# A Swin block on one core: epsilon moves into the summed squares, and the residual copy moves to another round

## The reference, cut to what matters

```python
def _ln(x, w, b):
    mu = x.mean(-1, keepdims=True)
    var = x.var(-1, keepdims=True)
    return (x - mu) / jnp.sqrt(var + 1e-05) * w + b
...
y = _ln(x, norm1_w, norm1_b)            # then roll and cut into windows
qkv = win @ qkv_w.T
attn = softmax(q @ k.T * scale + bias + mask)
x = shortcut + (attn @ v) @ proj_w.T + proj_b
z = _ln(x, norm2_w, norm2_b)
return x + gelu(z @ fc1_w.T + fc1_b) @ fc2_w.T + fc2_b
```

## Time and profile before

| what | value |
|---|---|
| median of 3 runs | 2193.38 us (2191.87 to 2196.89) |
| the profiled execution: time / span | 2191.34 us / 2189.5 us |
| PE / PEld busy | 2140.3 us (98%) / 1667.7 us (76%) |
| DVE / ACT / POOL busy | 1780.1 (81%) / 1545.3 (71%) / 1772.9 us (81%) |
| transfers | 165.86 MB, 76 GB/s |
| mean granted PE clock | 0.993 |

### The profile page before, as it was taken

How to read it: one execution, slowest core, us unless ns; L and a number is a source line. 1 busy time by engine, 2 the same in 40 slices (tenths; PEclk the granted TensorE clock), 3 DMA queues, 4 the chain that set the end, 5 groups by cost and what they waited for, 6 DMA issues and landing times.

```text
span 2189.5 us, 148006 instructions
## 1 busy us (share of the span) xinstructions
PE 2140.3 (98%) x62790; PEld 1667.7 (76%) x62790; DVE 1780.1 (81%) x3231; ACT 1545.3 (71%) x2435; POOL 1772.9 (81%) x1687
## 2 busy tenths in 40 slices
PE   6999999999999999999999999999999999999997
PEld 3777777777777777777777777777777777777775
DVE  5788888888888888888888888888888888888874
ACT  4577777677677777767777776776777777777774
POOL 5788888888888888888888888888888888888874
PEclk8999999999999999999999999999999999999999
DMA  4232233222323332232323223233223333322321
GB/s 111 65 78 78 75 75 76 77 77 76 79 74 76 76 76 77 75 79 76 77 76 76 77 75 77 78 75 79 75 77 77 76 77 76 77 76 76 77 70 32
DMA packets 178587, 165.86 MB, mean 76 GB/s; under 512 B 21144, under 2 KB 152458, under 8 KB 178074
## 3 DMA queue, kind: packets, MB, share of 16 engines
q1 hardware_dynamic: 178074, 157.60, 28.0%
HBM read 28.99 MB, written 25.77 MB: 25 GB/s over the span
## 4 chain that ended last, share of the span: by engine, by line
PE 88%; DVE 4%; issue 3%; ACT 2%; SPq 2%; DMA 1%; DVEq 0%; POOL 0%; ACTq 0%; POOLq 0%
PE O L758 14%; PE S L722 11%; PE ST L744 10%; PE M L766 9%; PE ST L738 9%; PE M L829 9%; PE M L851 8%; PE M L814 5%; PE M L798 5%; PE M L784 4%; PE M L859 2%; PE S L726 2%; SPq L274 1%; DVE nm L582 1%; ACT gl L445 1%
## 5 line engine op out<-in xcount | busy, mean ns | idle before, releaser
L326 POOL TENSOR_TENSOR nmd<-diag,nm 121x392 f16<-121x392 f16 x1024 | 900.3, 892 | 288.1 <-DVE nm L582 234.1
L582 DVE TENSOR_REDUCE nm<-S 121x8 f16<-121x392 f32 x1024 | 574.3, 561 | 225.7 <-PE S L722 138.3
L426 ACT ACTIVATE pT<-ST 113x392 f32<-113x392 f32 x1024 | 506.9, 496 | 229.7 <-PE ST L744 224.9
L758 PEld LDWEIGHTS O<-vx,pT 113*49 113x49 f32 x16384 | 548.6, 126 | 45.1 <-issue 6.1
L758 PE MATMUL O<-vx,pT 113*49 113x18 f32 x16384 | 522.2, 196 | 3.8 <-issue 1.9
L722 PE MATMUL S<-kp,qp 128*49 128x49 f16 x16384 | 390.7, 186 | 11.0 <-DVE nm L582 7.9
L738 PE MATMUL ST<-qp,kp 128*49 128x49 f16 x16384 | 387.0, 185 | 2.4 <-issue 2.3
L722 PEld LDWEIGHTS S<-kp,qp 128*49 128x49 f16 x16384 | 313.0, 103 | 93.1 <-issue 55.5
L744 PE MATMUL ST<-nmd,shiftw 121*49 121x392 f16 x2048 | 354.4, 342 | 0.2 <-POOL nmd L326 0.2
L738 PEld LDWEIGHTS ST<-qp,kp 128*49 128x49 f16 x16384 | 324.8, 103 | 10.2 <-issue 2.3
L407 ACT ACTIVATE hl<-M 128x784 f16<-128x784 f32 x128 | 105.5, 824 | 309.1 <-PE M L784 229.3
(11 more groups left out here) (90 smaller groups left out, 3369.2 us busy)
## 6 DMA issues: line engine op xcount, KB each, us to landing
qp<-hl SPq DMA_DIRECT2D x1024, 49.0 KB
kp<-hl SPq DMA_DIRECT2D x1024, 49.0 KB
xin<-in_x SPq DMA_DIRECT2D x256, 98.0 KB
out<-res SPq DMA_DIRECT2D x256, 98.0 KB
kp<-in_c_keys SPq DMA_DIRECT2D x4, 588.0 KB, 7.2
weights<-in_c_weights SPq DMA_DIRECT2D x1, 448.0 KB, 4.4
bias_t<-spread SPq DMA_DIRECT2D x2, 73.5 KB, 2.2
shiftw<-in_c_shift SPq DMA_DIRECT2D x1, 139.0 KB
```

Of the source, the lines that this page charges most:

```text
L326: nc.gpsimd.tensor_tensor(nmd[j % LAG][:], diag[:], nm[j % LAG][:].unsqueeze(2).broadcast_to([RM, 2 * 4, N]), ALU.mult).then_inc(s_nmd, 1)
L426: nc.scalar.activation(pT[j % LAG][:].rearrange("k w h q -> k (w h q)"), ST[0:R, j % 2, 0:HK], ACT.Exp).then_inc(s_e, 1)
L582: V.tensor_reduce(nm[j % LAG][:], S[0:RM, 0:HK].rearrange("q (h n) -> q h n", n=N), AX_X, ALU.max, negate=True).then_inc(s_nm, 1)
L758: mm = MM(O[W0 * w:W0 * w + N, (4 * p + hp) * VC:(4 * p + hp + 1) * VC], pT[j % LAG][:, w, hp, :], vx[r % RING][:, window + 2 * w, hp, :], ...
```

## The change

Both layer norms computed `ss = sum(square(y0))` over 64 channels on DVE, then `veps = ss / 64 + EPS` in a second small DVE instruction, then `rstd = veps ** -0.5` on POOL. Now ACT writes `square(y0 / 8)`, which is the square divided by 64, into a buffer of 65 columns; the 65th column is filled with EPS once at the start, and DVE's sum over 65 columns is the variance plus epsilon. The second DVE instruction, its buffer and its semaphore go, and POOL's power reads ss. The wait for POOL's reading of the buffer (`s_rs`) moves in front of the sum. Two small memsets are added to POOL's start, and DVE waits for POOL's memsets before its first calculation.

Apart from this, `keep_residual` moves in POOL's program from the front of round 0 to behind `shift_rows` of round 3.

```diff
-        sq1 = sb("sq1", [R, UP, C])
+        sq1 = sb("sq1", [R, UP, C + 1])
...
-        ZEROED = RING + 2
+        ZEROED = RING + 4
...
+            nc.gpsimd.memset(sq1[:, :, C:C + 1], EPS).then_inc(c_zero, 1)
+            nc.gpsimd.memset(sq2[:, :, C:C + 1], EPS).then_inc(c_zero, 1)
...
             def ln1_rstd(u):
-                pool.wait_ge(s_ve1, u + 1)
+                pool.wait_ge(s_ss1, u + 1)
                 if later(u):
                     pool.wait_ge(s_y1, u)
-                nc.gpsimd.tensor_tensor(rstd1[:], veps1[:], mhalf[:], ALU.pow).then_inc(s_rs1, 1)
+                nc.gpsimd.tensor_tensor(rstd1[:], ss1[:], mhalf[:], ALU.pow).then_inc(s_rs1, 1)
...
                 for k in range(U):
-                    if k == 0 and on_chip(i):
-                        keep_residual(i, m)
                     if on_chip(i):
                         shift_rows(i, k)
+                    if k == 3 and on_chip(i):
+                        keep_residual(i, m)
...
-                nc.scalar.activation(sq1[:], y0[:], ACT.Square).then_inc(s_sq1, 1)
+                nc.scalar.activation(sq1[:, :, 0:C], y0[:], ACT.Square, scale=float(C) ** -0.5).then_inc(s_sq1, 1)
...
+            dve.wait_ge(c_zero, ZEROED)
             dve.wait_ge(c_vec_in, 16)
...
             def ln1_var(u):
                 dve.wait_ge(s_sq1, u + 1)
+                if later(u):
+                    dve.wait_ge(s_rs1, u)
                 V.tensor_reduce(ss1[:], sq1[:], AX_X, ALU.add).then_inc(s_ss1, 1)
-                dve.wait_ge(s_ss1, u + 1)
-                if later(u):
-                    dve.wait_ge(s_rs1, u)
-                V.tensor_scalar(veps1[:], ss1[:], 1.0 / C, EPS, ALU.mult, ALU.add).then_inc(s_ve1, 1)
```

More of the change, by code:

```diff
@@ L90, in swin_block @@
         y0 = sb("y0", [R, UP, C])
-        sq1 = sb("sq1", [R, UP, C])
+        sq1 = sb("sq1", [R, UP, C + 1])
         ss1 = sb("ss1", [R, UP])
-        veps1 = sb("veps1", [R, UP])
         rstd1 = sb("rstd1", [R, UP])
@@ L109, in swin_block @@
         z0 = sb("z0", [R, UP, C])
-        sq2 = sb("sq2", [R, UP, C])
+        sq2 = sb("sq2", [R, UP, C + 1])
         ss2 = sb("ss2", [R, UP])
-        veps2 = sb("veps2", [R, UP])
         rstd2 = sb("rstd2", [R, UP])
@@ L148, in swin_block @@
         s_ss1 = sem("s_ss1")
-        s_ve1 = sem("s_ve1")
         s_rs1 = sem("s_rs1")
@@ L176, in swin_block @@
         s_ss2 = sem("s_ss2")
-        s_ve2 = sem("s_ve2")
         s_rs2 = sem("s_rs2")
@@ L349, in ln2_rstd @@
             def ln2_rstd(u):
-                pool.wait_ge(s_ve2, u + 1)
+                pool.wait_ge(s_ss2, u + 1)
                 if later(u):
                     pool.wait_ge(s_z1, u)
-                nc.gpsimd.tensor_tensor(rstd2[:], veps2[:], mhalf[:], ALU.pow).then_inc(s_rs2, 1)
+                nc.gpsimd.tensor_tensor(rstd2[:], ss2[:], mhalf[:], ALU.pow).then_inc(s_rs2, 1)
             def ln2_rows(u):
@@ L438, in square2 @@
                     act.wait_ge(s_ss2, u)
-                nc.scalar.activation(sq2[:], z0[:], ACT.Square).then_inc(s_sq2, 1)
+                nc.scalar.activation(sq2[:, :, 0:C], z0[:], ACT.Square, scale=float(C) ** -0.5).then_inc(s_sq2, 1)
             def gelu(u, c):
@@ L557, in ln1_var @@
                 dve.wait_ge(s_sq1, u + 1)
-                V.tensor_reduce(ss1[:], sq1[:], AX_X, ALU.add).then_inc(s_ss1, 1)
-                dve.wait_ge(s_ss1, u + 1)
                 if later(u):
                     dve.wait_ge(s_rs1, u)
-                V.tensor_scalar(veps1[:], ss1[:], 1.0 / C, EPS, ALU.mult, ALU.add).then_inc(s_ve1, 1)
+                V.tensor_reduce(ss1[:], sq1[:], AX_X, ALU.add).then_inc(s_ss1, 1)
             def evac_yT(u):
@@ L616, in ln2_var @@
                 dve.wait_ge(s_sq2, u + 1)
-                V.tensor_reduce(ss2[:], sq2[:], AX_X, ALU.add).then_inc(s_ss2, 1)
-                dve.wait_ge(s_ss2, u + 1)
                 if later(u):
                     dve.wait_ge(s_rs2, u)
-                V.tensor_scalar(veps2[:], ss2[:], 1.0 / C, EPS, ALU.mult, ALU.add).then_inc(s_ve2, 1)
+                V.tensor_reduce(ss2[:], sq2[:], AX_X, ALU.add).then_inc(s_ss2, 1)
             def evac_zT(u):
```

## The result

The changed kernel takes 2204.16 us (median of 5 runs, 2199.97 to 2205.15), the kernel before 2192.84 us (5 runs, 2190.74 to 2196.89). The ratio is 1.0055, 95% interval 1.0040 to 1.0069: slower by 0.55%, where -0.15% was forecast. It is the side of rival A, and its size.

What follows compares the result with a forecast made beforehand. PE, busy 98% of the span, was taken as the bound, with a 3.35 us chain from `shift` to `turn_y` covering removed waits. Terms -3.0 and -0.2 gave 2193.4 - 3.2 = 2190.2 us (-0.15%), range 2186 to 2204.

Steps and rivals of the forecast that it cites:

- rival A: Full port lock: `ln2_center` 0.44 us late, `fc1_low` 0.12 us late in each of 122 bodies, 2205 us; chance 0.21.
- the last one of `keep_residual`: Round 2: `low_parts` ends 0.31 us later at 1535.12, plus 0.05 us, just in time for `fc1_low`; steady cost 0.
- The wait at round 3: PE's 0.17 us wait before `scores` of round 3 goes, with nil gain in three bodies of four.
- rival B: `turn_y` moves up with PE, so the round 3 wait is all gained: 21 us, 2172.6 us; chance 0.05.
- `ln2_center` "near 1.0 us": Sign on DVE: `ln2_center` meets POOL's `shift_rows` of round 0 and takes near 1.0 us in place of 0.69.
- xres "near 1.3 us": Sign on POOL: the xres copy of `keep_residual`, 1.60 us at its old place, takes near 1.3 us.
- 0.2 forecast: At the start: POOL's first power follows the sum directly without the first norm's second DVE instruction; gain 0.2 us, once.
- The -3.2 us of the epsilon edit: Whole kernel: -3.0 us from every fourth body and -0.2 us at the start.
- the 3 us of every fourth body: 30 longer bodies, where `turn_y` comes later in PE's order, gain 0.10 us each, 3.0 us in all.
- every fourth body near 16.82 us: Sign: the longer bodies with more mask matmuls shorten from 16.92 us to near 16.82 us.
- the risk at `fc1_low`: Round 2: each 0.1 us that `low_parts` comes later still delays `shift`, 12 us over 122 bodies.
- 0.01 us of room: Round 2: margin left before `fc1_low` at 1535.18, with `low_parts` at 1535.12 plus 0.05 us making 1535.17.

Runs made afterwards that it cites:

- experiment 2: The kernel before with only `keep_residual` moved behind `shift_rows` of round 3, variance step kept: 2201.62 us, ratio 1.0057.
- experiment 7: experiment 1 with an unused DVE sum over 312 elements in front of `low_parts`: 2204.01 us, ratio 1.0068 to the kernel before.
- Experiment 6: experiment 1 with an unused DVE sum over 52 elements in front of `low_parts`: 2185.90 us, ratio 0.9989 to the kernel before.
- experiment 9: experiment 1 with PE's `turn_y` of round 4 placed between `shift` and `times_v`: 2182.67 us, ratio 0.9961 to the kernel before.
- experiments 4: The changed kernel with POOL's old wait for `result` back in front of `shift_rows` of round 0: 2188.68 us, ratio 0.9993 to the kernel before.
- experiment 5: The changed kernel with `shift_rows` of round 0 as two instructions of half the size: 2189.97 us, ratio 0.9991 to the kernel before.
- experiment 1: The changed kernel with `keep_residual` back in front of round 0, leaving the epsilon columns alone: 2187.93 us, ratio 0.9992 to the kernel before.
- experiment 8: experiment 1 with PE's `turn_y` of round 4 moved behind `times_v`: 2231.87 us, ratio 1.0198 to the kernel before.

## Why the prediction was wrong

**The step that failed.** It is the last one of `keep_residual`: "`fc1_low` starts at 1535.18 and needs `low_parts` about 0.05 us before. It is just in time". The sum there was 0.31 us of delay plus 0.05 us of handover, against 0.37 us of room (1535.18 - 1534.81). Measured: the delay of `ln2_center` is 1.03 - 0.69 = 0.34 us, and the handover from the end of hl to `fc1_low` is 0.15 us, in the changed kernel, in experiment 2 and in experiment 7. The sum is 0.49 us, 0.12 us over the room, and this is what each ordinary body has become longer by. The larger error is the handover, 0.10 us. The 0.05 us came from `neg_max` to `scores`, another pair of instructions, and was taken over to this one unchecked. It holds in nearly every body: the median is 0.15 us over the ordinary bodies of all three kernels. Experiment 6 confirms the room that follows, 0.37 - 0.15 = 0.22 us: 0.1 us of it can be used for nothing.

**Where the 0.15 us come from.** `scores` waits for one semaphore in rounds 1 to 3, and its first weight load carries that wait. `fc1_low` waits for two. Its weight load carries the wait for zT; the one for `low_parts` (`s_lo`, L830 of the changed kernel) is an instruction of its own in PE's order (PEldq is the sequencer of PE's weight loads; times in ns):

```profile
L830 PEldq EVENT_SEMAPHORE  x124: 51/51/51, 89.1 to 2139.7; - x124
```

In body 90 it starts at 1539.82, 0.05 us after the end of hl, and takes its 0.05 us; the weight load follows at 1539.90 and the matmul at 1539.93. That the extra instruction matters, and not the engine or the operation that produces the data, is seen in two other places. At the end of the kernel before, where `low_parts` has no work left and zT comes last, the same `fc1_low` starts 0.05 us after the end of zT (2172.87):

```profile
2172.19 0.68 DVE L627 TENSOR_SCALAR zT<-M,vec 128x392 f32<-128x392 f32 x1
2172.92 1.59 PE L829 MATMUL M<-zT,weights 64*128 64x392 f32 x8 [1.13 <-DVE zT L627]
```

And behind an ACT activation `turn_y`, with two waits, starts 0.15 us after the first `gelu` (median of the changed kernel), while `scores_T`, with one, starts 0.05 us after the exp (experiment 9). This is read from the traces; no run changed the number of waits.

**Rival A had the place, the price and the time, but not the mechanism.** It gave 0.12 us a body and 2205 us; both came. It got there by 0.44 us of delay, by a hold for POOL's full instruction with all 0.69 us behind it, and 0.05 us of handover. The delay was 0.34 us. Two errors of 0.10 us cancel in it, so that its number came is luck. The Trainium skill, SBUF — State Buffer, "Who interferes with whom", has the hold and that the first one wins, which experiments 4 and 5 show. Full blocking is not what the 1.03 us shows, which would be 0.49 + 0.69 = 1.18 us. (The page writes of the whole instruction, and of full blocking, where it speaks of DVE's two-port modes; of two SBUF inputs it says that they contend. The prediction put the two together.)

**What held.** The wait at round 3 went (0.54 us behind `shift`), and nothing of it was gained in ordinary bodies, because `turn_y` stays 3.34 us behind `shift`; experiment 1 shows it alone, and rival B is out. `ln2_center` "near 1.0 us" came as 1.03, xres "near 1.3 us" as 1.27. At the start POOL's first power begins 0.18 us earlier, for 0.2 forecast:

```profile
2.66 0.11 POOL L300 MEMSET sq<- 113x8 f32 x1
...
16.75 1.64 POOL L331 TENSOR_TENSOR rstd<-ss,mhalf 113x8 f32<-113x8 f32 x1 [4.63 <-DVE ss L559]
```

The new memsets take 0.11 us each, and ACT's scaled squares and the wider sum cost nothing that shows. The -3.2 us of the epsilon edit fit experiment 1 (0.9985 lies in its interval), but that interval also holds no change: the 3 us of every fourth body are not shown by the times. The traces show them in experiment 1 (16.93 to 16.81 us, medians). In the changed kernel they did not come: there the late `fc1_low` takes 0.16 us from these bodies too, more than the gain, and the sign "every fourth body near 16.82 us" failed with 16.98. The forecast counted the gain of the fourth bodies and the risk at `fc1_low` apart.

**The choice that failed.** The forecast rested on 0.01 us of room, and the text said so, but it gave the case beyond that edge a chance of 0.21 and set the upper end of the range at 2204, below rival A's own 2205 and within the result's spread (2199.97 to 2205.15). The two terms of the sum were off by 0.03 and 0.10 us, where it had 0.01 us to spare; both sides of the edge should have had the same weight.

**What stays open.** Each profile has some bodies that are longer than the median, by up to 1.6 us. They come in all kernels, add up to some 8 us in the trace before and 5.5 us in the one after, and were not looked into. This is why the medians of the bodies give 13 us in all (92 x 0.125 and 31 x 0.05) where the traces differ by 10.1.

## What to carry to other kernels

Work taken off an engine frees it earlier, and then it meets something new: before moving a step away, look for what its neighbours will overlap with in its absence, and for whether two instructions on DVE and POOL both read two tensors from SBUF. Where a sum leaves a hundredth of a microsecond, read each handover from the very pair of instructions it is for, look at how many semaphores the waiting group has, and treat the forecast as undecided. A wait on the busiest engine can be a cover for another one (experiments 1, 8 and 9): before removing it, find which wait is next, and follow the order past it.

## What the runs showed of the hardware

- A DVE instruction with two SBUF inputs that starts while a POOL tensor_tensor runs ends 0.54 to 0.56 us after that one's end, in place of 0.69 us after its own start (1.03 us in all in the changed kernel, 0.71 us behind the half instruction of experiment 5). If the DVE instruction starts first it keeps its 0.68 us, and POOL's is stretched (0.51 to 0.96 us for the half one).
- POOL's copy of 113x512 takes 1.60 us beside `ln2_center` and 1.27 us where it is alone.
- Not every meeting of the two counts: in body 90 of the changed kernel `low_parts`, with one input in PSUM (M) and one in SBUF, takes its usual 0.96 us, and POOL's `shift_rows`, which starts 0.24 us after it, its usual 0.84 us.
- From the end of the producer to the start of the PE group that waits for it: 0.15 us where that wait is a separate instruction in PE's order (hl to `fc1_low`, 1539.78 to 1539.93; `on` to `times_v` in experiment 8; the first `gelu` to `turn_y`), 0.05 us where the weight load carries it (`neg_max` to `scores`; zT to `fc1_low`; exp to `scores_T` in experiment 9). DVE and ACT are among the producers of both kinds.
